# Windowed attention in units of one tile and four heads: the value product one unit later, two buffers for what it reads, and the projections copied behind the exps

## What is computed

```python
def attn0(x, w_qkv, w_out):               # x: (8, 512, 128), 16 heads of 64, window 32
    xn = x * rsqrt(mean(x * x, -1) + 1e-6)
    q, k, v = split(xn @ w_qkv.T)          # each (8, 16, 512, 64)
    q, k = rope(q, cos, sin), rope(k, cos, sin)
    attn = einsum('bhqd,bhkd->bhqk', q, k) / 8
    attn = where((q_pos >= k_pos) & (q_pos - k_pos <= 32), attn, -1e9)
    attn = softmax(attn)
    out = einsum('bhqk,bhkd->bhqd', attn, v)
    return merge_heads(out) @ w_out.T

x = x + ga * attn0(layernorm(x) * (1 + ca) + sa, ...)
# then: expert feed-forward, second attention (2 heads, full), quantised feed-forward
```

## Time and profile before

| | us |
|---|---|
| median of 3 runs | 1297.09 (1296.6 to 1300.16) |
| span of the profiled execution | 1295.1 |
| TensorE busy | 975.8 (75%) |
| VectorE busy | 805.3 (62%) |
| ScalarE busy | 639.2 (49%) |
| GpSimd busy | 430.4 (33%) |

### The profile page before, as it was taken

How to read it: one execution, slowest core, us unless ns; L and a number is a source line. 1 busy time by engine, 2 the same in 40 slices (tenths; PEclk the granted TensorE clock), 3 DMA queues, 4 the chain that set the end, 5 groups by cost and what they waited for, 6 DMA issues and landing times. The chain is left out here.

```text
span 1295.1 us, 25137 instructions
## 1 busy us (share of the span) xinstructions
PE 975.8 (75%) x8604; PEld 662.5 (51%) x8604; DVE 805.3 (62%) x1683; ACT 639.2 (49%) x2132; POOL 430.4 (33%) x332
## 2 busy tenths in 40 slices
PE   6779998989899999985613769747348787867665
PEld 3456565656656565664503556534225454545454
DVE  5777758687777767564657514112136878559995
ACT  3565767767676767671101323112038777643322
POOL 2334333333342423321000857886611312200221
PEclk9789899999999998987555789888759999868967
DMA  6564343434443434431402123445310000000000
GB/s 198 150 182 107 92 123 88 119 96 113 102 113 100 113 83 107 104 91 42 102 0 62 45 59 69 61 73 129 31 66 1 1 2 1 1 1 9 17 17 25
DMA packets 89009, 93.62 MB, mean 72 GB/s; under 512 B 18800, under 2 KB 62304, under 8 KB 88944
## 3 DMA queue, kind: packets, MB, share of 16 engines
q1 hardware_dynamic: 78576, 84.12, 24.7%
q0 software_dynamic: 10368, 8.66, 4.7%
HBM read 24.36 MB, written 10.70 MB: 27 GB/s over the span
## 5 line engine op out<-in xcount | busy, mean ns | idle before, releaser
L835 POOL TENSOR_TENSOR qk_cos<-qk_raw,const 128x512 f32<-128x512 f32 x128 | 183.2, 1432 | 313.0 <-ACT qk_raw L589 313.0
L575 ACT ACTIVATE prob<-psS,neg_max 128x96 f32<-128x96 f32 x512 | 167.9, 342 | 86.5 <-DVE neg_max L670 85.7
L442 PE MATMUL psQ<-a_xnT,weights 128*128 128x512 f32 x250 | 146.0, 668 | 2.1 <-ACT a_xnT L621 1.4
L550 PEld LDWEIGHTS psO<-probT,v_windows 96*64 96x64 f32 x2048 | 73.7, 143 | 142.6 <-ACT probT L649 121.1
L550 PE MATMUL psO<-probT,v_windows 96*64 96x64 f32 x2048 | 91.8, 235 | 43.9 <-ACT probT L649 43.9
L685 DVE TENSOR_TENSOR qk_roped<-qk_cos,qk_swapped 128x512 f32<-128x512 f32 x128 | 119.0, 929 | 5.9 <-DVE qk_swapped L676 5.5
L1508 POOL DMA_INDIRECT sums<-ex_y,ex_index x64 | 97.6, 1525 | 39.5 <-issue 23.5
L1497 POOL DMA_INDIRECT ex_rows<-rows,ex_index x64 | 67.1, 1048 | 121.8 <-DMA ex_index<-lists 102.6
L575 ACT ACTIVATION_READ_ACCUMULATOR prob<-psS,neg_max 128x1 f32 x512 | 105.4, 206 | 0.0
L1442 ACT ACTIVATE ex_hidden<-ex_psH,ex_b 128x512 f32<-128x512 f32 x64 | 43.7, 687 | 114.4 <-PE ex_psH L1401 59.7
L649 ACT COPY probT<-psT 96x512 f32<-96x512 f32 x128 | 76.8, 600 | 46.5 <-PE psT L530 46.5
(11 more groups left out here) (317 smaller groups left out, 1936.2 us busy)
## 6 DMA issues: line engine op xcount, KB each, us to landing
qk_swapped<-qk_raw SPq DMA_DIRECT2D x512, 64.0 KB, 2.0
v_windows<-v_tok SPq DMA_DIRECT2D x32, 384.0 KB, 4.4
v_windows<-v_tok SPq DMA_DIRECT2D x32, 256.0 KB, 3.6
mod<-mod_rows SPq DMA_DIRECT2D x12, 512.0 KB, 6.0
ex_w<-in_L_ffn_W SPq DMA_DIRECT2D x16, 256.0 KB
v_windows<-v_tok SPq DMA_DIRECT2D x32, 96.0 KB, 2.1
rows<-rt_h SPq DMA_DIRECT2D x8, 256.0 KB, 2.4
sums<-rt_zeros SPq DMA_DIRECT2D x8, 256.0 KB, 2.7
```

The source lines that it names most:

```text
L442: last = nc.tensor.matmul(bank, k.wqkvT[:, col:col + P], xnT[:, :], start=True, stop=True)
L550: ins = nc.tensor.matmul(psO[D * j:D * j + D, i * P + a * HALF:i * P + (a + 1) * HALF], vw[:, par, a, t, hd], probT[:, 2 * j + i, a * HALF ...
L575: last = nc.scalar.activation(prob[:, s, 2 * j + i, :], psS[:, s, j, i * KW:(i + 1) * KW], ACT.Exp, bias=nmax[:, s, 2 * j + i:2 * j + i + ...
L835: nc.gpsimd.tensor_tensor(rcos[:, half, :], raw[:, half, :], k.const[:, K_COS:K_COS + T], ALU.mult).then_inc(cos_done, 1)
```

## The change

In unit u TensorE no longer multiplies unit u's probabilities with the values but unit u-1's (`apply(b, u - 1)`); unit 15's product comes after three quarters of the output projection, and the last quarter of that moves into unit 0 of the next batch. `probT` and `v_tok` get a second buffer, and with it `v_placed` becomes two semaphores. ScalarE copies `oT` two units late, and takes the exps right behind the `probT` copy, ahead of both pieces. SyncE swaps first and places the windows in tile 1 instead of tile 0. The room for the buffers comes from the modulation's weights, which now lie in a tensor that is filled later.

```diff
-        self.w, self.sgn, self.mag = sb("w", [C, MODS * C]), sb("sign", [B, C]), sb("mag", [B, C])
+        self.w = sb("w", [C, MODS * C]) if layer else k.mod1[:, 0, 0:MODS, :].rearrange("p b c -> p (b c)")
...
-        v, vw = sb("v_tok", [P, TILES, 4 * D]), sb("v_windows", [KW, 2, 2, TILES, 4 * D])
+        v, vw = sb("v_tok", [P, 2, TILES, 4 * D]), sb("v_windows", [KW, 2, 2, TILES, 4 * D])
-        probT = sb("probT", [KW, 4, P])
+        probT = sb("probT", [KW, 2, 4, P])
...
+            def apply(b, u):
+                n, g, t = b * UNITS + u, u // TILES, u % TILES
+                wait(pe, probT_ready, n + 1)
+                wait(pe, oT_ready, n)
+                if t == 0:
+                    wait(pe, v_placed[g % 2], (b * (QUADS // 2) + g // 2 + 1) * 48)
...
+                    if u == 0 and not begins:
+                        wait(pe, oT_ready, b * UNITS)
+                        out_project(b - 1, [PAIRS - 2, PAIRS - 1], False, True)
                     if not (last and u + 2 >= UNITS):
                         score(b, u + 2)
...
-                    if u == 8 and not last:
-                        wait(pe, xnT_ready, b + 2)
+                    if u == 8:
+                        apply(b, u - 1)
+                        if not last:
+                            wait(pe, xnT_ready, b + 2)
                     for q, m in pieces[:1]:
                         project(b, q, m)
...
+                    if u not in (0, 8):
+                        apply(b, u - 1)
                     for q, m in pieces[1:]:
                         project(b, q, m)
...
                 out_project(b, list(range(PAIRS - 2)), True, False)
-                wait(pe, oT_ready, b * UNITS + UNITS)
-                out_project(b, [PAIRS - 2, PAIRS - 1], False, True)
+                apply(b, UNITS - 1)
+                if last:
+                    wait(pe, oT_ready, b * UNITS + UNITS)
+                    out_project(b, [PAIRS - 2, PAIRS - 1], False, True)
...
-                    if u > 0:
-                        copy_oT(b, u - 1)
+                    if u >= 2:
+                        copy_oT(b, u - 2)
                     wait(act, turned, b * UNITS + u + 1)
-                    nc.scalar.copy(probT[:, :, :], psT[0:KW, :, :]).then_inc(probT_ready, 1)
-                    pieces = pieces_at(g, t, last)
-                    for q, m in pieces[:1]:
-                        piece(b, q, m)
+                    nc.scalar.copy(probT[:, u % 2, :, :], psT[0:KW, :, :]).then_inc(probT_ready, 1)
                     if not (last and u + 2 >= UNITS):
                         exps(b, u + 2)
-                    for q, m in pieces[1:]:
+                    for q, m in pieces_at(g, t, last):
                         piece(b, q, m)
...
-                    if t == 0 and not (last and g + 1 >= QUADS):
-                        wait(sp, oT_ready, b * UNITS + g * TILES)
-                        windows(g + 1)
                     q, half = ahead(u, 8)
                     if not (last and q >= QUADS):
                         swap(b, q, half)
+                    if t == 1 and not (last and g + 1 >= QUADS):
+                        if last:
+                            sp.wait_ge(piece_out, (b * QUADS + g + 2) * PIECES)
+                        wait(sp, applied, b * UNITS + g * TILES)
+                        windows(g + 1)
```

36 lines of the change are left out of this document (17 added, 19 removed).

## The result

The changed kernel takes 1411.84 us in the median of four runs (1403.16 to 1420.59) against 1298.62 us for the kernel before beside it: a ratio of **1.087** [1.0817, 1.0923]. It is slower by 113 us. The profiled execution is the fastest of the four, 1403.16 us with a span of 1401.4 us (before 1295.1). Ratios, here and in the experiments, are of the fast runs alone, which leaves out one of 1367.17 us in experiment 3 and one of 1337.25 us of the kernel before.

What follows compares the result with a forecast made beforehand. The prediction took the ring, not TensorE, to bound the kernel. First batch +13, six middle batches +78.3 and last +6.2 made +97.5 on the 1295.1 us span, 1392.6; with 2.0 to the median, 1394.6 us, range 1380 to 1425.

Steps and rivals of the forecast that it cites:

- The ring: ScalarE and VectorE chain from exps through reciprocal, division, sines and maxima to next exps: 3.31 us, 4.20 in tile 1.
- what waits outside the ring: Middle batch's 15 rounds: 4.4 us beyond the ring's 53.2, the most the later value product could gain.
- VectorE's other work fits too: VectorE between maxima and next reciprocal: the next batch's norm was said to fit into 2.0 us.
- faster: Rival: neither port nor swaps hold the sines, rounds run at their floor; 1279 us, chance 0.05.
- Exps ahead of the pieces: ScalarE order: cosines ask at E+1.94, ahead of the sines; rounds with cosines get 1.07 us longer, 4.38 and 5.27.
- the lower one (cosines beside the division): Bound: cosines run beside VectorE's division, so a round's excess is 0.94 us, not 1.07; 15 us less in all.
- Value product one unit later: TensorE: removes the 0.74 us wait for probT, new waits fall into slack; gain at most 4.4 us per batch, swallowed.
- the batch's end: Last exps to next batch's first: 12.4 us against 10.97, 1.4 lost, as out_project waits for late piece 4.
- SyncE: Swaps start 1.8 us later in a round but land before their sines; cost 0, thin cover in tile 2.
- Transfers: Rival: GpSimd does not hold up the sines and late swaps pace the ring; 1331 us, chance 0.10.
- Slower clock: Rival: TensorE at half clock through half of the output projections; +33 over the forecast, 1427 us, chance 0.10.
- No change: Rival: blocked sines in only a few rounds, cancelling the gain; 1297 us, chance 0.02.

Runs made afterwards that it cites:

- experiment 3: Changed kernel with one wait added on GpSimd: the cosines wait until VectorE's maxima of the next unit are done; 1346.7 us, ratio 1.0348.
- experiment 5: Changed kernel with the first piece copied ahead of the exps again and the cosines waiting for VectorE's maxima; 1300.61 us, ratio 1.0044.
- experiment 6: Kernel before with one wait added on GpSimd: the cosines wait for VectorE's maxima; 1292.19 us, ratio 0.9968.
- experiment 9: experiment 5 with the output projection in one piece behind the last value product and unit 8's product behind its projection; 1306.44 us, ratio 1.0079.
- Experiment 1: Kernel before with only ScalarE's order changed, the exps ahead of both pieces; 1382.76 us, ratio 1.0657.
- experiment 8: The changed kernel as it is, traced a second time in one execution; 1414.03 us.
- experiment 2: Changed kernel with one edit undone, the first piece copied ahead of the exps again; 1322.02 us, ratio 1.0192.

## Where the prediction was right and where it was not

**What bounds the kernel.** The time came inside the range, and what made the rounds longer is what was forecast. The ring was the right thing to follow. Its floors of 3.31 and 4.20 show up in every version in which cosines leave the sines and tile 1's rotation alone and VectorE keeps its order (experiments 5, 6, 9). The reading of the other 4.4 us per batch as "what waits outside the ring" that the later product could win was wrong in its last part, since the later product does not win them: experiments 5, 6 and 9 show 57.2 to 58.1 us for 15 rounds, not 53.2. Of the 4.4 us, 3.8 are in the first half of a batch, where VectorE has the residual and the next batch's norm (its rounds there, in the kernel before: 4.20, 3.31, 3.59, 4.03, 5.11, 3.88, 3.75, 4.21). "VectorE's other work fits too" was a step that failed: the 2.0 us between maxima and reciprocal were not held against rows of that work, which takes up to 1.76 and 2.11 us when the cosines fall on it (experiment 5), behind a rotation of 0.68. The kernel before has such cases: the instruction at 276.21, of 1.76 us, pushes the reciprocal behind it to 277.90, 0.72 us late, and its round is 4.03 and not 3.31; a rotation of 1.68 us at 279.64 and the norm's statistics behind it do the same to the round of 5.11. It cost the sum nothing here, since at 4.38 a round there was room. It did cost the rivals: no version came near the "faster" of 1279 us.

**Exps ahead of the pieces.** Right to 0.02 us in each of these links: cosines at E+1.95 (forecast 1.94), sines issued 0.17 us later (0.19), ended at E+3.88 (3.89), rounds 4.38 and 5.27 (4.38 and 5.27), 15 rounds 69.39 (69.3). Experiment 1 shows that this edit alone does it, and experiment 3 that it does it through GpSimd's meeting with VectorE. Of the bounds, the lower one (cosines beside the division) did not come. The rule of the Trainium skill that the prediction weighed (page "SBUF — State Buffer", section "Who interferes with whom") is borne out by the 1.76 us of the sines.

**Value product one unit later.** Right that TensorE's wait for `probT` goes and that the rounds show nothing of it. But TensorE did not come to wait for normalised probabilities, as the signs had it: it stands idle 45.7 us in all ahead of the value products, as before (43.9), now mostly put down to "issue", and 6.8 us ahead of the transposes. Wrong that it costs nothing where it lands: the price is at the batch's end, 1.35 us of the 1.68 there (11.30 to 12.65 between experiment 1 and the changed kernel). The prediction's sum of 12.4 for the batch's end held this price, but laid the loss on the late piece, which costs 0.33 (10.97 to 11.30). It also said that the split of the projection hides nothing; experiment 9 shows 1.1 us hidden by it.

**The batch's end.** 12.65 against 12.4. The two parts of the projection took 5.62 + 2.05 = 7.67 us, where I had scaled 7.14 to 5.36 and 1.79.

**SyncE.** Zero was right for the rounds of the profiled execution, and the cover was as thin as said. Some sines started late for their swap, one at E+3.16 (365.30 us) and not E+2.12, and still ended at E+3.88; in experiment 8 three rounds got 0.2 to 0.6 us longer by it, and with the sines free the swaps are late (experiment 3). In the first batch it was not zero. There one swap is late in both kernels, and in the changed one by more; VectorE waits 9.25 us for it, before 5.37 (both lines below, the kernel before first). These 3.9 us are more than the 3.0 missing between the first batch's +13 and +16.0. The traces of the experiments narrow down where they come from: the same wait is 4.59 us with the exps moved alone (experiment 1) and 3.57 to 5.37 in all six traces that keep SyncE's order and the value product of before, 7.97 to 9.96 in all six with both changed. Which part of the change does it wasn't tried.

```profile
84.71 0.69 DVE L676 TENSOR_TENSOR qk_swapped<-qk_swapped,const 128x512 f32<-128x512 f32 x1 [5.37 <-DMA qk_swapped<-qk_raw]
93.13 0.69 DVE L687 TENSOR_TENSOR qk_swapped<-qk_swapped,const 128x512 f32<-128x512 f32 x1 [9.25 <-DMA qk_swapped<-qk_raw]
```

**The sum.** Forecast against measured (last `y_mul`): first batch +13 and +16.0; six middle batches +78.3 and +83.7; last +6.2 and +7.55. The middle ones without the long batch are 82.04 x 6 = 492.2, less the 416.4 of before, +75.9; before had two longer batches of its own (71.95, 70.01) which the forecast's 6 x 68.6 left out; each holds 6.8 us in which TensorE was granted half its clock (from 146.1 and from 490.9 us), with a round of 5.11 us where the other batches have 3.75. The stop of TensorE adds 7.5. The median of the changed kernel is 8.7 us above the profiled execution; the second trace, at 1414.03 us, has two stops, so more stops are the likely reason, but the slower executions have no traces. Stops are the term that the prediction lacks. Without them both traces stand at 1395, the time forecast, and to the microsecond that is luck: the first batch and the last are 4.4 us above their terms, the middle ones 2.4 below theirs, and behind the last `y_mul` 0.9 us come back.

**The rivals.** Transfers: not in the changed kernel, but next in line (experiment 3). Faster: its condition (the sines issue before the cosines ask) was missed by 0.17 us, and experiment 5, which has the cosines ask later, is at 1300.61 and not at 1279: VectorE's other work, with the cosines falling on it, is the limit then. Slower clock: TensorE was granted 0.96 over a middle batch, and full clock in the projection at its end (first two rows below). Half clock came behind the stop (third row), where 16 matmuls took 3.57 us instead of 2.05; that is part of the 7.5 us. It came in the rounds too, 3.4 or 6.8 us at a time and two or three times in each of the later middle batches (from 371.9 and from 416.3 us, for instance), where the kernel before has none from 153 to 490 us; the rounds there are as long as the others. The slack that takes this up is smaller than the prediction's "over 2 us": its own 18.4 and 13.7 us for four units leave 1.2 us a round. What the rival describes did happen once elsewhere: in experiment 9, 3.4 us at half clock fell on the last value product and the projection of a middle batch, whose end was 14.55 us and not 13.06. No change: out.

```profile
382.00:388.00 6.00, 5.51 (x48) 5.43 (x48) 0.73 (x2) 1.20 (x3) 1.38 (x1) 1.00 0.23 59
388.00:391.40 3.40, 3.40 (x44) 2.98 (x43) 0.00 (x0) 0.95 (x2) 0.00 (x0) 1.00 0.00 0
303.00:310.00 7.00, 4.58 (x33) 4.12 (x34) 0.62 (x2) 0.58 (x1) 0.00 (x0) 0.54 0.01 2
```

**What stays open.** Why TensorE stops at some batch boundaries and not at others. The stops stand where the loop over middle batches goes from one pass to the next. There are five in the twelve traces, all in kernels with the whole change (the changed kernel one and two, experiment 3 two), and each comes with nine packets of instruction fetches, four of them at the boundary. In all five the transposes start 1.74 to 1.76 us behind the end of one packet and the output projection 1.38 to 1.50 behind the end of the next; the other boundaries between two passes have one packet at most. So TensorE waits there for something that comes with the fetches; no run takes the fetches away, and what calls for them is open. Of the 0.3% of experiment 6 a part can be named: 2.8 of the 3.2 us between the two profiled spans lie in one batch near the start (71.95 to 69.11). There the kernel before has a rotation of tile 1 that meets the cosines (1.48 us at 127.63, 0.69 with the wait), and the round is 5.46 and not 4.20. Most of the rest falls where the kernel before had 6.8 us at half clock (from 146.1 us) and experiment 6 had 3.4 (from 143.0), which is not the wait's doing as far as is known.

## What to carry over

Before moving work on an engine that only seems to wait, list what each moved instruction sets off on the other engines and at what offset from the ring's first instruction it now asks; here a copy moved from ahead of the exps to behind them let GpSimd ask 0.17 us ahead of VectorE, and a round at its floor got 1.07 us longer. A second buffer could pay only if the buffer were on the ring, and here it was not: follow one round from start to start through all engines first, and put against its slack the longest work that must fit there, with the length it has when another engine holds it up. And cure a collision where it arises: one added wait that keeps the disturber away gave back 65 us. Then look where the disturber went, since here it met the residual, the norm or the rotation instead.

## What the hardware showed that was not expected

Who is held up, and by how much, depends on who asks first. GpSimd's cosines, asking 0.31 us after the division had begun, took 1.38 us against 1.28 alone, so they lost 0.10; the sines behind them lost 1.07. With the rotation in the earlier trace rows GpSimd had lost 0.46. In both cases, the one at 275.69 and the one at 423.32, the cosines end 1.28 us after a point 0.14 to 0.15 us ahead of the recorded end of the VectorE instruction (276.15 and 423.42), so VectorE seems to let go a little before its row ends. That is worked out from two meetings, not tested. Nor is it only instructions with two tensors as input that lose: the four of L302, which read one tensor with a mean and a scale, took 2.11 us with the cosines beside them and 1.10 without (experiments 5 and 2).

A program can also lose time at a loop's boundary without any row of an engine that names a cause: the batches with a stop are 7.5 to 10.5 us longer in the changed kernel, the kernel before has no stop, and what shows them is the queue of instruction fetches (37, 46, 55 packets, and their times). Between the two traced executions of 1403 and 1414 us the stops make the difference, and not the rounds, which are 4.38 and 5.27 in both but for the three named; for the execution of 1420 us there is no trace. The other difference between batches of one kernel is the granted clock: 6.8 us at half clock in a batch of the kernel before made one round 1.4 us longer, where TensorE had no slack.
